# Causal masks added by VectorE in PSUM, and both 1024-row products in three parts from weights fetched in turn

## The chip, the cores and the metric

The kernel runs on one core of a Trainium2 chip. The metric is the device time of one execution in microseconds (us), from start to end, median of three runs.

## The reference

`x` is [64, 256, 256] and `ctx` is [64, 77, 256], all float32. For each of the 64 batches the reference computes two layers:

```
# layer 0: cross-attention over 77 keys, 16 heads of 64
n  = x * rsqrt(mean(x*x) + 1e-6) * norm_w
x  = x + softmax((n @ wq) (ctx @ wk)^T) (ctx @ wv) @ wo          # wo is [1024, 256]
# layer 1: causal attention, cross-attention, MLP; 16 heads of 16
x  = x + mha(ln1(x), ln1(x), causal=True) @ m_proj_w + m_proj_b
x  = x + mha(ln2(x), ctx,    causal=False) @ c_proj_w + c_proj_b
x  = x + relu(ln3(x) @ f_w1 + f_b1) @ f_w2 + f_b2                # f_w2 is [1024, 256]
```

In the causal attention a score whose key comes after its query is minus infinity before the softmax.

## The kernel before

A batch is cut into about a hundred **steps**, named as in the order table: `stat`, `norm`, `turn` (statistics, normalised rows, transposes), `q0 k0 v0` and `q1 k1 v1` (projections), `qs0` (layer 0 scores of one query tile and four heads, query rows down the partitions, for the softmax sums), `mt` (transposed shifts), `sk0` (the same scores with keys down the partitions, for the probabilities), `pv0` (probabilities times values), `wo` (output product, one of two row tiles); for the causal attention `qsA` and `qsB` (scores of query tile 0 and 1, for the sums), `skA` and `skB` (scores for the probabilities), `pv.1`, `proj.1`; for the third attention `qs2`, `sk2`, `pv.2`, `proj.2`; for the MLP `h.0` to `h.3` (256 hidden rows each) and `f2` (one of two row tiles). `ln.k` takes the logarithm of the sums of softmax k.

`LOOP_ORDER_TEXT` is one turn of the steady loop as a single row of steps. A turn works on three batches at once; the suffix `-` or `+` says that a step belongs to the older or to the younger of them. All engines walk this one row, each doing its own part of a step, so the row sets the order on TensorE (PE), ScalarE (ACT), VectorE (DVE) and GpSimd (POOL). 62 of the 64 batches' turns run in that loop; shorter rows fill and empty the pipeline.

The eight PSUM banks are dealt out in turn: a step takes the next one, two or four banks of the ring. `full[s]` counts what PE put into bank s and `free[s]` what was taken out; PE waits on `free` before it writes.

**Products.** float32 data goes through PE in one of two ways. `three` (lines 841 to 843) uses operands that were split into a high and a low float32r part and makes three matmuls. `plain_rows_product` (line 876) multiplies float32 as it is; the trace shows each such matmul as two. `wo` and `f2` use the plain way: eight k-slices of 128, each 128x128 by 128x256, for each of two row tiles. `wo0` and `wf2` lie in SBUF all the time; `coT` holds layer 0's attention output and, later in the turn, the hidden activations `hT`. ScalarE writes both: `pv0` by a copy from PSUM, `h` by a Relu with bias (line 575).

**Masks.** PE adds the causal mask to the scores by a bf16 matmul of an identity and a mask tile: line 958 after `qsA`/`qsB`, line 1009 ahead of `skA`/`skB`, one for each of the four banks of a step.

**Softmax sums.** DVE takes the maxima of a bank (line 701), ACT then exponentiates each head's piece with an accumulated sum (line 480, each followed by a read of the accumulator). The probabilities are plain exponentials of a whole bank (lines 549, 553, 557).

**Setup.** SP loads small tiles, `wk0`, `ck`, `wo0`, `f2`, and then the ten weights of `WEIGHTS` one after the other through two staging areas, where DVE splits them (lines 616 to 624). Nothing of the batches starts before DVE has given `consts_ready`.

## Time and profile before

| | |
|---|---|
| median of 3 runs | 5340.66 us (5338.04 to 5346.11) |
| the profiled execution | 5337.84 us, its span 5336.1 us |
| PE busy | 5106.7 us, 96% of the span |
| ACT busy | 4342.2 us, 81% |
| DVE busy | 2212.1 us, 41% |
| POOL busy | 536.4 us, 10% |
| granted TensorE clock | 0.993 of full speed |
| DMA | 67.10 MB, mean 13 GB/s |

Busy means that at least one instruction of the engine was under way. Matmuls are pipelined: a row in the trace lasts until its modelled end, while the next one starts earlier. What a kind of matmul costs PE is therefore read from the distance of the starts, and a duration is not added up.

### The profile page before, as it was taken

Reading aid. Unit: us, or ns where it says so; the run is one execution under the profiler, and the core shown is the slowest. Engines: PE = TensorE matmul, PEld = TensorE weight load, DVE = VectorE, ACT = ScalarE, POOL = GpSimd, SP = SyncE. Lnnn points to the kernel's source line nnn. Section 1 sums busy time; section 2 is a strip of 40 time slices with the busy share of each in tenths; the row PEclk is TensorE's granted clock in tenths of the full one; section 3 lists DMA queues with packets and bytes.
Section 4 is the critical chain, followed back from the end, with each engine's and each line's share of the span. In section 5 each row is a group of like instructions: output and inputs, shape, how many; then the busy total and the mean of one; then the engine's idle time right before and its main releaser. Section 6 shows DMA issues by size and latency. Waiting matters only on the chain.

```text
span 5336.1 us, 138120 instructions
## 1 busy us (share of the span) xinstructions
PE 5106.7 (96%) x48328; PEld 4133.6 (77%) x48328; DVE 2212.1 (41%) x5823; ACT 4342.2 (81%) x17665; POOL 536.4 (10%) x845
## 2 busy tenths in 40 slices
PE   6999999999999999999999999999999999999996
PEld 5777777787787777777777777877777777777775
DVE  3444444443444444444444444434444444444442
ACT  3888888888888888888888888888888888888884
POOL 0001011111111011010110111110110100101100
PEclk9999999999999999999999999999999999999998
DMA  2000000000000000000000000000000000000000
GB/s 76 12 8 14 13 8 13 13 8 13 12 9 13 10 11 13 8 13 13 8 14 13 8 14 13 8 13 10 11 13 8 13 13 8 14 13 7 14 8 5
DMA packets 64257, 67.10 MB, mean 13 GB/s; under 512 B 4593, under 2 KB 62769, under 8 KB 63921
## 3 DMA queue, kind: packets, MB, share of 16 engines
q1 hardware_dynamic: 63920, 64.19, 3.9%
q14 instruction: 318, 2.60, 0.2%
q8 instruction: 19, 0.31, 0.0%
HBM read 47.40 MB, written 16.78 MB: 12 GB/s over the span
## 4 chain that ended last, share of the span: by engine, by line
PE 62%; ACT 24%; DVE 6%; issue 6%; DMA 0%; DVEq 0%; POOL 0%; ACTq 0%; SPq 0%; PEldq 0%; PEld 0%; POOLq 0%
PE ps L876 17%; ACT ps L480 15%; PE ps L841 6%; PE ps L843 5%; PE ps L842 5%; PE ps L1048 5%; PE ps L1031 4%; ACT coT L575 3%; PE ps L1020 3%; PE ps L929 3%; PE ps L1009 2%; PE ps L997 2%; PE ps L939 2%; PE ps L1015 2%; ACT v L460 2%
## 5 line engine op out<-in xcount | busy, mean ns | idle before, releaser
L480 ACT ACTIVATE ps<-ps,negmax 128x77 f32<-128x77 f32 (+2 forms) x6144 | 2076.8, 397 | 197.0 <-DVE negmax L701 195.4
L480 ACT ACTIVATION_READ_ACCUMULATOR ps<-ps,negmax 128x1 f32 x6144 | 1617.6, 275 | 0.8
L701 DVE TENSOR_REDUCE negmax<-ps 128x4 f32<-128x308 f32 (+2 forms) x1792 | 923.5, 563 | 765.8 <-PE ps L939 381.3
L433 POOL TENSOR_TENSOR small<-small 128x1 f32<-128x1 f32 (+1 forms) x448 | 260.9, 582 | 4608.3 <-DVE small L675 2305.7
L696 DVE TENSOR_TENSOR zTl<-ps,zTh 128x256 fp32r<-128x256 f32 x512 | 199.3, 420 | 898.0 <-ACT zTh L460 898.0
L876 PE MATMUL ps<-wf,coT 128*128 128x256 f32 x2048 | 475.8, 386 | 46.4 <-ACT coT L575 46.4
L876 PEld LDWEIGHTS ps<-wf,coT 128*128 128x128 f32 x2048 | 379.8, 190 | 127.0 <-issue 80.2
L876 PE MATMUL ps<-wo,coT 128*128 128x256 f32 x2048 | 475.9, 385 | 0.0
L557 ACT ACTIVATE probs<-ps 128x512 f32<-128x512 f32 x768 | 394.9, 601 | 70.1 <-PE ps L1020 70.1
L876 PEld LDWEIGHTS ps<-wo,coT 128*128 128x128 f32 x2048 | 378.6, 190 | 66.7 <-issue 10.3
L549 ACT ACTIVATE probs<-ps 77x512 f32<-77x512 f32 x512 | 275.5, 588 | 182.2 <-PE ps L981 179.1
L929 PE MATMUL ps<-k0bd,q0T 128*128 128x154 f32 x2048 | 310.7, 299 | 0.0
L553 ACT ACTIVATE probs<-ps 77x512 f32<-77x512 f32 x512 | 254.6, 602 | 62.2 <-PE ps L997 62.2
L841 PE MATMUL ps<-xTh,hi_wq 128*128 128x256 f32 x1024 | 299.2, 292 | 1.5 <-DVE xTl L696 1.5
L841 PE MATMUL ps<-zTh,hi_f 128*128 128x256 f32 x1024 | 290.2, 283 | 1.0 <-issue 1.0
L843 PE MATMUL ps<-xTh,lo_wq 128*128 128x256 f32 x1024 | 287.4, 281 | 0.0
L842 PE MATMUL ps<-xTl,hi_wq 128*128 128x256 f32 x1024 | 286.8, 280 | 0.0
L843 PE MATMUL ps<-zTh,lo_f 128*128 128x256 f32 x1024 | 284.7, 278 | 0.0
L842 PE MATMUL ps<-zTl,hi_f 128*128 128x256 f32 x1024 | 284.7, 278 | 0.0
L929 PEld LDWEIGHTS ps<-k0bd,q0T 128*128 128x128 f32 x2048 | 277.2, 190 | 8.8
L981 PE MATMUL ps<-q0T,k0bd 64*77 64x256 f32 x2048 | 263.6, 376 | 0.0
L912 PEld LDWEIGHTS ps<-cT,wk 128*128 128x128 f32 x2048 | 243.4, 192 | 9.0
(181 smaller groups left out, 10798.5 us busy)
## 6 DMA issues: line engine op xcount, KB each, us to landing
xin<-x_dram SPq DMA_DIRECT2D x64, 256.0 KB, 2.7
x<-x_dram SPq DMA_DIRECT2D x64, 256.0 KB, 2.7
out<-xr SPq DMA_DIRECT2D x64, 256.0 KB, 2.3
cin<-ctx_dram SPq DMA_DIRECT2D x64, 77.0 KB
wk<-wk_dram SPq DMA_DIRECT2D x1, 1024.0 KB, 5.1
wo<-wo_dram SPq DMA_DIRECT2D x1, 1024.0 KB, 7.9
wf<-f_dram SPq DMA_DIRECT2D x1, 1024.0 KB, 10.3
probs<-wq_dram SPq DMA_DIRECT2D x1, 1024.0 KB, 9.6
```

Of the source, the lines that this page charges most:

```text
L433: nc.gpsimd.tensor_tensor(rstd[:, stage, ts], veps[:, stage, ts], minus_half[:, ts], ALU.pow).then_inc(rstd_ready[stage], 1)
L480: ins = nc.scalar.activation(scores, scores, ACT.Exp, bias=negmax[w][:, t, h:h + 1], accum_out=sums[w][:, t, h:h + 1])
L549: nc.scalar.activation(probs_slot(step, e)[0:S], bank(s)[0:S, :], ACT.Exp).then_inc(free[s], 1)
L557: nc.scalar.activation(probs_slot(step, r), bank(s), ACT.Exp).then_inc(free[s], 1)
L701: nc.vector.tensor_reduce(dst, bank(s)[:, 0:heads * width].rearrange("p (h k) -> p h k", h=heads), AX_X, ALU.max, negate=True).then_inc(ma ...
L841: pe.matmul(o, lh, rh, start=first, stop=False)
L842: pe.matmul(o, lh, rl, start=False, stop=False)
L843: return pe.matmul(o, ll, rh, start=False, stop=last)
L876: ins = pe.matmul(bank(s)[:, 0:C], src[:, k, t * P:(t + 1) * P], weight[:, k, :], start=(k == 0), stop=(k == kt - 1))
L929: ins = pe.matmul(bank(s)[:, j * 2 * S:(j + 1) * 2 * S], q0T[:, m, t * P:(t + 1) * P], k0bd[:, m, :, :], start=True, stop=True)
L981: ins = pe.matmul(bank(s)[0:S, j * T:(j + 1) * T], k0bd[es, m, e, :], q0T[es, m, :], start=False, stop=(j == 1), skip_group_check=True)
L1048: ins = pe.matmul(bank(s)[rows, 0:T], lhs, p, start=(e == 0), stop=(k == 2 and e == 1), skip_group_check=True)
```

## The change

1. **Masks.** The mask matmuls go. DVE adds the mask tile to the scores in PSUM, in place, bank by bank (`mask`): before the maxima in `qsA` and `qsB` (semaphore `chain`), before ACT's exponential in `skA` and `skB` (semaphore `masked`).
2. **Both 1024-row products in three parts.** `wo` and `f2` become `tail_product`, which uses `three`. Their left operands are split: `coTh` and `coTl`. For `pv0`, ACT writes the high part and DVE the low one; for `h`, DVE makes both parts and ACT has no share any more. The two weights, split, no longer fit side by side: one pair of tiles `tail_h`, `tail_l` holds one of them at a time. Setup splits both and stores the parts in DRAM (`parted`); in every turn POOL fetches 2 MB of `f2` parts after `wo.1`, and 2 MB of `wo` parts after `f2.1`. The Relu is max(y, -bias) with the bias moved into the row that `f2` adds.
3. **Orders.** A new order of steps; ACT and DVE get orders of their own, in which the parts of a step (a bank, a mask `m0` to `m3`, a half of `h`) are placed singly.
4. **Banks.** Each step names its banks in the table (`:4156`), in place of the ring.
5. Layer 0's probabilities get four slots in place of eight. SP's loads follow the order of steps. One turn of the loop is written out, so the loop runs 61 times.

```diff
-    mt.0- rms+ pv.1.1 sk0.3- proj.1.1 proj.1.0 sk0.1- sk0.2- sk0.0- stat.2.0 stat.2.1 norm.0+ norm.2.0
...
+mt.0-:7 pv.1.1:1 sk0.1-:23 proj.1.1:6 proj.1.0:1 stat.2.0 sk0.0-:75 stat.2.1 norm.2.0 norm.2.1 rms+ pv0.1-:2
...
+def signals(order):
...
-        wo0 = sb("wo0", [P, M0, C])
-        wf2 = sb("wf2", [P, MF, C])
+        tail_h, tail_l = sb("tail_h", [P, M0, C], F32R), sb("tail_l", [P, M0, C], F32R)
...
+            def store_parts(n, value):
+                i = [m for m, _, _ in WEIGHTS].index(n)
+                sp.wait_ge(w_free[i % 2], i // 2 + 1)
+                sp.dma_start(parted[n][0], tail_h[:].bitcast(F32)).then_inc(parts_out, 16)
+                sp.dma_start(parted[n][1], tail_l[:].bitcast(F32)).then_inc(parts_out, 16)
+                sp.wait_ge(parts_out, value)
...
+            def load_parts(kind):
+                n = "wo0" if kind == "wo" else "f2"
+                nc.gpsimd.dma_start(tail_h[:], parted[n][0]).then_inc(tail_in[kind], 16)
+                nc.gpsimd.dma_start(tail_l[:], parted[n][1]).then_inc(tail_in[kind], 16)
...
+                    if n in ("wo", "f2") and (n, 1 - step[1]) in c.seen:
+                        done = {s: v for st in order if st[0] == n for s, v, _ in c.of[st]["bank"]}
+                        for s, v in done.items():
+                            pool.wait_ge(full[s], v)
...
+                        nc.gpsimd.tensor_tensor(passed[:], minus_half[:], minus_half[:], ALU.mult)
+                        if later:
+                            load_parts(later[0])
...
+            def mask(u, r, heads, tile, at, added):
+
+                s, v, _ = u["bank"][r]
+                dve.wait_ge(full[s], v)
+                scores = bank(s).rearrange("p (h k) -> p h k", h=heads)[:, :, at:at + P]
+                nc.vector.tensor_tensor(scores, scores, tile[:].unsqueeze(1).to_broadcast([P, heads, P]),
+                                        ALU.add).then_inc(added, 1)
...
+                            ins = nc.vector.tensor_scalar(hTh[:, k, :], bank(s)[:, m * T:(m + 1) * T],
+                                                          minus_bias[:, k:k + 1], None, ALU.max)
...
+                            ins = nc.vector.scalar_tensor_tensor(out=hTl[:, k, :], in0=bank(s)[:, m * T:(m + 1) * T],
+                                                                 scalar=minus_bias[:, k:k + 1],
+                                                                 in1=hTh[:, k, :].bitcast(F32), op0=ALU.max,
+                                                                 op1=ALU.subtract)
...
-            def plain_rows_product(u, weight, src, kt, t):
+            def tail_product(u, th, tl, t):
                 s = take_bank(u)
-                for k in range(kt):
-                    ins = pe.matmul(bank(s)[:, 0:C], src[:, k, t * P:(t + 1) * P],
-                                    weight[:, k, :], start=(k == 0), stop=(k == kt - 1))
+                ts = slice(t * P, (t + 1) * P)
+                for k in range(M0):
+                    ins = three(bank(s)[:, 0:C], th[:, k, ts], tl[:, k, ts], tail_h[:, k, :], tail_l[:, k, :],
+                                k == 0, k == M0 - 1)
                 ins.then_inc(full[s], 1)
...
-                        for s, _, _ in u["bank"]:
-                            heads = 4 if n == "qsA" else 2
-                            diagonal = bank(s).rearrange("p (h k) -> p h k", h=heads)[:, :, 512 // heads - P:]
-                            pe.matmul(diagonal, identb[:], causal[:].unsqueeze(1).to_broadcast([P, heads, P]),
-                                      start=False, stop=True, skip_group_check=True).then_inc(full[s], 1)
```

**Three places in the loop.** On DVE, behind the statistics of the layer norm ahead of the MLP (`stat.3`). Before, the rows there are:

```order
L665 BN_STATS stats<-xs 128x6 [waits free0]
L660 REGISTER_ALU
L669 BN_AGGR mv<-stats 128x2 [waits chain]
L660 REGISTER_ALU
L678 TENSOR_SCALAR small<-mv 128x1 [waits chain]
L682 REGISTER_ALU
L687 TENSOR_SCALAR z<-xs,mv,small 128x256 [waits rstd_ready1]
L682 REGISTER_ALU
L687 TENSOR_SCALAR z<-xs,mv,small 128x256 [waits rstd_ready1]
L694 REGISTER_ALU
L696 TENSOR_TENSOR zTl<-ps,zTh 128x2x128 [waits hi_done]
L694 REGISTER_ALU
```

They are the statistics, the two normalised tiles (`z`) and the low parts of their transposes. Now there stand:

```order
L760 BN_STATS stats<-xs 128x6 [waits free2]
L755 REGISTER_ALU
L764 BN_AGGR mv<-stats 128x2 [waits chain]
L755 REGISTER_ALU
L773 TENSOR_SCALAR small<-mv 128x1 [waits chain]
L805 REGISTER_ALU
L806 TENSOR_REDUCE negmax0<-ps 128x4 [waits full1]
L804 REGISTER_ALU
L806 TENSOR_REDUCE negmax1<-ps 128x2 [waits full4,chain]
L777 REGISTER_ALU
L782 TENSOR_SCALAR z<-xs,mv,small 128x256 [waits rstd_ready1]
L796 REGISTER_ALU
```

Between the second statistics and its normalised tile there are now a `qs0` maximum and a `qsB` one, and masks follow.

On PE, around the first tile of `f2` (`L929` and `L1061` are `qs0` scores). Before:

```order
L929 MATMUL ps<-k0bd,q0T 128x154 [waits free4,free1]
L929 MATMUL ps<-k0bd,q0T 128x154
L876 MATMUL ps<-wf2,coT 128x256 [waits free4,free2,free3,free1]
L876 MATMUL ps<-wf2,coT 128x256 x7
L837 REGISTER_ALU
L1009 MATMUL ps<-identb,causal 128x2x128 [waits free3,free7]
L1009 MATMUL ps<-identb,causal 128x2x128 [waits free4]
L1009 MATMUL ps<-identb,causal 128x2x128 [waits free5]
L1009 MATMUL ps<-identb,causal 128x2x128 [waits free6]
L1015 MATMUL ps<-maxT1,head_of32 128x256 x8
```

Now:

```order
L1061 MATMUL ps<-k0bd,q0T 128x154 [waits free0,free2]
L1061 MATMUL ps<-k0bd,q0T 128x154
L225 REGISTER_ALU
L1061 MATMUL ps<-k0bd,q0T 128x154 [waits free0,free3,free7]
L1061 MATMUL ps<-k0bd,q0T 128x154
L1206 ISA [waits free5,free3]
L972 MATMUL ps<-tail_h,coTh 128x256 [waits free6,f2_in]
L973 MATMUL ps<-tail_l,coTh 128x256
L974 MATMUL ps<-tail_h,coTl 128x256
L972 MATMUL ps<-tail_h,coTh 128x256
```

The plain matmuls and the mask matmuls of `skA` behind them are gone; `f2` waits for the fetched weights (`f2_in`) and for the banks that DVE frees.

On POOL, where `wo.1` ends. Before:

```order
L433 TENSOR_TENSOR small<-small 128x1 [waits stat_ready2]
L452 TENSOR_TENSOR x1<-x1,row 128x256 [waits norm_ready2]
L432 REGISTER_ALU
L433 TENSOR_TENSOR small<-small 128x1 [waits stat_ready2]
L452 TENSOR_TENSOR x1<-x1,row 128x256 [waits norm_ready2]
L432 REGISTER_ALU
```

Now:

```order
L517 TENSOR_TENSOR small<-small 128x1 [waits stat_ready2]
L548 ISA
L548 ISA [waits full1]
L553 TENSOR_TENSOR passed<-small 128x2 [waits full0]
L522 DMA tail_h<-parted_f2 128x2048
L523 DMA tail_l<-parted_f2 128x2048
L544 TENSOR_TENSOR x1<-x1,row 128x256 [waits norm_ready2]
```

Ahead of the row additions POOL now waits until both `wo` tiles are in their banks and issues two DMAs.

## Rows read from the trace of the kernel before

**Rows 1.** Page, part 1: busy us (share of span) xinstructions.

```profile
span 5336.1 us, 138120 instructions
...
PE 5106.7 (96%) x48328; PEld 4133.6 (77%) x48328; DVE 2212.1 (41%) x5823; ACT 4342.2 (81%) x17665; POOL 536.4 (10%) x845
```

**Rows 2.** Busy us by engine in a turn, from `qsA` to `skB`, and behind `qs2.1`.

```profile
core 0: us, PE busy (x) PEld busy (x) DVE busy (x) ACT busy (x) POOL busy (x), PEclk, DMA share, GB/s
2674.24:2755.36 81.12, 79.07 (x758) 64.04 (x754) 34.12 (x90) 67.73 (x276) 8.33 (x13) 1.00 0.03 11
2713.09:2745.26 32.17, 30.98 (x280) 25.11 (x278) 14.96 (x34) 28.65 (x125) 2.50 (x4) 1.00 0.01 3
2690.53:2702.68 12.15, 12.15 (x88) 10.88 (x85) 6.91 (x21) 11.10 (x67) 1.84 (x3) 1.00 0.00 1
```

**Rows 3.** Timeline, SP: start us, us, engine line op; one turn apart.

```profile
2674.24 0.40 SPq L400 DMA_DIRECT2D out<-xr  x1
...
2755.36 0.40 SPq L400 DMA_DIRECT2D out<-xr  x1
```

**Rows 4.** Timeline, PE: start, us, operation xcount [idle before <-releaser].

```profile
2715.40 0.28 PE L841 MATMUL ps<-hi_cp,zTh 128*128 128x256 f32 x1
...
2716.46 0.28 PE L841 MATMUL ps<-hi_mv,z1Th 128*128 128x256 f32 x1
...
2727.58 0.61 PE L958 MATMUL ps<-causal,identb 128*128 128x256 bf16 x4
2727.94 0.37 PE L841 MATMUL ps<-zTh,hi_f 128*128 128x256 f32 x1
...
2737.40 3.69 PE L876 MATMUL ps<-wf,coT 128*128 128x256 f32 x16 [0.73 <-ACT coT L575]
2740.93 0.60 PE L1009 MATMUL ps<-identb,causal 128*128 128x256 bf16 x4
2741.45 0.51 PE L1015 MATMUL ps<-maxT,head_of 32*128 32x256 f32 x8
...
2742.76 1.04 PE L1009 MATMUL ps<-identb,causal 128*128 128x512 bf16 x4
2743.72 0.67 PE L1015 MATMUL ps<-maxT,head_of 32*128 32x128 f32 x16
...
2745.26 2.37 PE L929 MATMUL ps<-k0bd,q0T 128*128 128x154 f32 x16
```

**Rows 5.** Timeline, all engines, softmax sums behind `qs2.1`, up to its `mt.2`.

```profile
2691.13 0.30 ACT L480 ACTIVATE ps<-ps,negmax 128x77 f32<-128x77 f32 x1 [0.65 <-DVE negmax L701]
...
2701.41 0.23 ACT L542 ACTIVATE logs<-sums 128x32 f32<-128x32 f32 x1 [0.37 <-ACT ps L480]
...
2702.16 0.29 DVE L755 TENSOR_TENSOR mparts<-negmax,mparts 128x128 fp32r<-128x128 f32 x1
...
2702.68 0.38 PE L965 MATMUL ps<-ident,mparts 128*128 128x128 f32 x2
```

**Rows 6.** Groups by line and form: xcount | busy us, mean ns | idle before.

```profile
L696 DVE TENSOR_TENSOR zTl<-ps,zTh 128x256 fp32r<-128x256 f32 x512 | 199.3, 420 | 898.0 <-ACT zTh L460 898.0
...
L696 DVE TENSOR_TENSOR xTl<-ps,xTh 128x512 fp32r<-128x512 f32 x64 | 44.2, 691 | 51.6 <-ACT xTh L460 51.6
...
L557 ACT ACTIVATE probs<-ps 128x512 f32<-128x512 f32 x768 | 394.9, 601 | 70.1 <-PE ps L1020 70.1
...
L575 ACT ACTIVATE coT<-ps,bias_h 128x256 f32<-128x256 f32 x512 | 192.8, 485 | 6.3 <-PE ps L843 6.3
```

**Rows 7.** DMA issues: KB each, us to landing.

```profile
wo<-wo_dram SPq DMA_DIRECT2D x1, 1024.0 KB, 7.9
wf<-f_dram SPq DMA_DIRECT2D x1, 1024.0 KB, 10.3
```

**Rows 8.** Timeline, setup: last weight split, ACT's table load behind `consts_ready`.

```profile
49.48 0.76 DVE L624 SCALAR_TENSOR_TENSOR lo_cp<-probs,hi_cp 128x256 fp32r<-128x256 f32 x2
...
53.44 1.28 ACT L586 ACT_TABLE_LOAD   x1 [53.44 <-DVEq L654]
```

More of the change, by code:

```diff
@@ L17 @@
 MASKED = -1e30
-RINGS = {"bank": 8, "split": 1, "chain": 1, "max": 1}
+RINGS = {"bank": 8, "split": 1, "chain": 1, "max": 1, "masked": 1}
 FIRST = 24
@@ new lines @@
+skA.0/1 skA.0/2 skA.0/0 skA.0/3 skB/3 skB/0 skB/1 skB/2 qs0.1.1 qs0.1.0 ln.0 pv.1.0 skA.1/3 skA.1/2 skA.1/1
+skA.1/0
+"""
+DVE_ORDER_TEXT = """
+pv.1.1 proj.1.1 proj.1.0 stat.2.0 stat.2.1 norm.2.0 pv0.1 norm.2.1 rms turn.2.1 pv0.0 turn.2.0 norm.0 pv0.3
+pv0.2 qs2.1/3 qs2.1/1 qs2.1/2 turn.0 qs2.1/0 wo.0 stat.1.0 qs2.0/2 qs2.0/3 qs2.0/0 qs2.0/1 wo.1 norm.1.0
+stat.1.1 ln.2 norm.1.1 turn.1.0 turn.1.1 pv.2.0 pv.2.1 ctx qsA/m0 qsA/0 qsA/m3 qsA/m1 qsA/3 qsA/1 qsA/m2
+proj.2.0 stat.3.0 qsA/2 qsB.0/m3 qsB.0/m2 qsB.0/m0 qsB.0/3 qsB.0/2 qsB.0/m1 qsB.0/0 norm.3.0 proj.2.1
@@ L52, in steps, with step_of @@
+stat.3.1 qs0.1.2 qsB.0/1 norm.3.1 qsB.1/m1 qsB.1/1 qsB.1/m3 qsB.1/3 turn.3.1 turn.3.0 qsB.1/m0 qsB.1/m2
+qs0.0.2 qs0.0.0 qsB.1/0 qsB.1/2 h.2/0 h.2/1 h.0/0 qs0.0.1 ln.1 qs0.1.3 h.0/1 h.1/0 qs0.0.3 h.1/1 skA.0/m1
+skA.0/m2 skA.0/m0 skA.0/m3 h.3/0 h.3/1 skB/m3 skB/m0 skB/m1 skB/m2 qs0.1.1 qs0.1.0 f2.0 ln.0 pv.1.0 skA.1/m3
+skA.1/m2 skA.1/m1 skA.1/m0 f2.1
+"""
+def step_of(word):
+    name, *numbers = word.split(".")
+    return (name, *map(int, numbers))
 def steps(text):
-    order, stages = [], {}
+    order, stages, banks = [], {}, {}
@@ L54, in steps, with parts_of @@
     for word in text.split():
-        name, *numbers = word.rstrip("+-").split(".")
-        step = (name, *map(int, numbers))
+        word, _, taken = word.partition(":")
+        step = step_of(word.rstrip("+-"))
         order.append(step)
         stages[step] = {"+": 2, "-": 0}.get(word[-1], 1)
-    return order, stages
-LOOP_ORDER, STAGES = steps(LOOP_ORDER_TEXT)
+        banks[step] = [int(c) for c in taken]
+    return order, stages, banks
+def parts_of(text):
+    items = []
+    for word in text.split():
+        word, _, part = word.partition("/")
+        items.append((step_of(word), int(part) if part.isdigit() else part))
+    return items
@@ L113 @@
 CARRIED = [(p, step) for step in LOOP_ORDER for p in sources(step) if (STAGES[p] + 1) % 3 < (STAGES[step] + 1) % 3]
-def slot_uses(order):
-    total = {r: sum(USES[step[0]].get(r, 0) for step in order) for r in RINGS}
-    return {r: [(total[r] - s + n - 1) // n for s in range(n)] for r, n in RINGS.items()}
+def signals(order):
+    inside = set(order)
+    given = {r: [] for r in RINGS}
+    for step in order:
+        assert len(BANKS[step]) == USES[step[0]].get("bank", 0)
+        given["bank"] += [(step, j, s) for j, s in enumerate(BANKS[step])]
+    for step, _ in ACT_ORDER:
+        if step in inside and "split" in USES[step[0]]:
+            given["split"].append((step, 0, 0))
+    for step, part in DVE_ORDER:
+        uses = USES[step[0]]
+        if step not in inside:
+            continue
+        if "masked" in uses:
+            given["masked"].append((step, int(part[1:]), 0))
+        elif str(part).startswith("m"):
+            given["chain"].append((step, int(part[1:]), 0))
+        elif "max" in uses:
+            given["max"].append((step, part or 0, 0))
+        elif "chain" in uses and part != 1:
+            given["chain"] += [(step, j, 0) for j in range(uses["chain"])]
+    return given
@@ L151, in all @@
-    def all(self, order):
-        for step in order:
-            self.next(step)
-        return self
+        self.after = after
+        self.of = {step: {"place": k, **{r: [None] * n for r, n in USES[step[0]].items()}} for k, step in enumerate(order)}
+        self.seen = set()
+        for ring, given in signals(order).items():
+            at = [0] * RINGS[ring]
+            for step, j, s in given:
+                at[s] += 1
+                value, total = before[ring][s] + at[s], sum(before[ring]) + sum(at)
+                if per_turn is not None:
+                    value = turn * per_turn[ring][s] + value
+                    total = turn * sum(per_turn[ring]) + total
+                self.of[step][ring][j] = (s, value, total)
```

285 lines of the change are left out of this document (156 added, 129 removed).

## Prediction

> **What bounds the kernel now.** I read the page's busy shares first: PE is busy for 96% of the span, ACT for 81%, DVE for 41% [rows 1]. The span is 5336.1 us. Next comes the period of the steady loop. The store of a finished batch is issued once a turn, and two of these issues stand 81.12 us apart [rows 3], so 62 turns make 5029 of the 5336 us. The window of such a turn says how full it is: PE 79.07 us, ACT 67.73, DVE 34.12, at full clock [rows 2]. PE lacks work for 2.05 us of a turn. That is a PE bound, with ACT 13 us behind it. Busy shares over a turn hide where ACT is as good as full, though, so I looked at two stretches. From `qsA` to `skB` (32.17 us) PE is busy for 30.98 and ACT for 28.65; 1.19 of PE's 2.05 us of waiting lie here, 0.73 of them ahead of `f2.0`, which waits for ACT's Relu [rows 2, 4]. Behind `qs2.1` (12.15 us up to `mt.2`) PE is never idle, but the chain it would wait for next ends just in time: the last `mparts` is written at 2702.45, `mt.2` starts at 2702.68 [rows 2, 5].
>
> **The change part by part.** All terms are per turn, against 81.12 us.
>
> *Tail products.* One tile of `f2` costs PE 3.53 us (2737.40 to 2740.93) [rows 4]; four tiles make 14.1. In three parts, a k-slice is three matmuls; such slices start 0.353 us apart (2715.40 to 2716.46 is three of them, with data as the stationary operand as here) [rows 4]. 4 tiles x 8 slices x 0.353 = 11.3. PE saves 2.8 us.
>
> *Mask matmuls.* A group of four 512 wide takes PE 0.96 us (2742.76 to 2743.72), one 256 wide between 0.36 (2727.58 to 2727.94) and 0.52 (2740.93 to 2741.45) [rows 4]. Two of the first and four of the second kind at 0.44: 3.7 us saved.
>
> PE's own work falls from 79.07 to 72.6 us. With the waits of today the turn would be 74.6 us.
>
> *ACT* loses `h`: 192.8 us over 64 batches, 3.0 a turn [rows 6]. The copy of `pv0` becomes a rounding copy of the same size. ACT's work becomes 64.7 us.
>
> *DVE* gains masks (8 of 512 columns at 0.69 us, 16 of 256), the two parts of `h` (16 of 256), and `pv0`'s low parts (4 of 512). 256 columns are 0.42 us singly and 0.38 in a row (two in 0.76) [rows 6, 8]. 12 x 0.69 + 32 x 0.38 = 20.4; DVE reaches 54.5 us. Its in-place adds in PSUM are in no row of before; I price them by the subtractions that read PSUM and write SBUF, and bound them by 0.34 (half) and 1.0 us for 512 columns.
>
> So over a whole turn PE stays the fullest. The two stretches decide.
>
> *The stretch from `qsA` to `skB`.* The new order has the same steps here except that `f2.0` comes behind it, and four more `qs0` and one `q0` come into it. PE: 30.98 - 3.53 - masks 3.2 (two 512, three 256) + 2.4 for four `qs0` [rows 4] + 1.4 for a `q0` (twelve matmuls of 0.118) = 28.1 us. ACT: 28.65 - 3.0 + 16 exponentials of 77 columns + 0.6 for `q0`'s copy + 2.1 for `skB`'s four. The 77-wide ones run at 0.31 us (32 of them from 2691.13 to 2701.04, which is 0.37 before the logarithm) [rows 5], so 5.0; `skB`'s are 394.9/768 = 0.51 each [rows 6]. Sum 33.3. DVE: 14.96 + masks 8 x 0.69 + 12 x 0.38 + `h` 16 x 0.38 + four maxima at about 0.4 = 32.7. Both are longer than PE. `f2.0` needs `h.3`'s low part, which DVE makes after all of this except `skB`'s masks (2.8): not before 29.9, plus about 1 us before DVE has its first bank of `qsA`. So PE waits 1.8 us at least and some 2.9 with that lag, most of it at the new order's `turn.3` (DVE's normalised tile stands behind two maxima), `mt.1` and `f2.0`. Within DVE's 32.7 us no further gap is allowed for; with `chain` waits between a mask and its maximum I get up to 4.0. I take 2.7, nearer to the bare sum, since steps can slip past each other, where 1.19 stood.
>
> *Behind `qs2.1`.* PE's 12.15 us become 12.15 - 1.4 (two `wo` tiles) + about 0.2 (`turn.1.0`) = 10.9. The chain (maxima, 32 exponentials, logarithm, `mparts`) is untouched and took 2690.53 to 2702.45, 11.9 us [rows 5]. PE now waits 1.1 us where it waited 0. Bounds: 0 if ACT finds its scores earlier, 1.5.
>
> *Elsewhere* the waits stay: 2.05 - 1.19 = 0.86.
>
> Period: 72.6 + 2.7 + 1.1 + 0.86 = 77.2 us, 3.9 less. 62 turns: -242 us. The two batches' worth of work outside the steady turns save PE's 6.5 each: -13.
>
> *Weight fetch.* The store of a batch is issued at 2674.24, and `wo.0` starts at 2690.53 [rows 2, 3], 16.3 us later; `f2.1` ended some 0.8 us ahead of the store (DVE's add of 0.42 and two hand-overs), so there are 17.1 us for a fetch in the place of before, and 15.7 after, since one `q0` is moved out. The second of two 1 MB loads landed 7.9 us after its issue, the third 10.3 [rows 7]. Two loads by POOL then need about 8 to 10 us plus POOL's own work of 1 to 3. I cost it at nothing, under cover of those 15.7 us; each us beyond them costs 62. The `f2` fetch has over 35 us. POOL's row additions behind `wo.1` come later by its issue time, ahead of work that PE needs several us later: nothing. The loads are issued by POOL and change dtype to float32r. The Trainium skill, "DMA: Bandwidth & Descriptors", section "SWDGE vs HWDGE vs iDMA", has it that GpSimd writes the descriptors into SBUF rings and can be locked out of them by VectorE's two-port mode, which would speak against a fetch by POOL beside a busier VectorE; the same page ("Anatomy of one DMA") gives 2.0 us plus bytes over 436 GB/s, an estimate of 6.8 us for both MB, by which the fetch would be early. No row of before shows a DMA of POOL's, so neither can be weighed here, and the sum would be the same by the second.
>
> *Setup.* Splitting two more weights: 2 x 8 slices x 2 parts at 0.38 = 12 us at most [rows 8]; storing one's parts before the other may be split: 8 (two 1 MB, as the 7.9 row); bias rows and the wait for a load: 4; two 1 MB loads fewer ahead of the first weight: -5. Sum +19, between 8 and 30. All of it lies ahead of the first batch.
>
> Span: 5336.1 - 242 - 13 + 19 = 5100. The median of before is 4.6 above the profiled span, so I predict **5105 us**.
>
> **The rivals.**
>
> *The waits don't grow.* If the new orders and the fixed banks let ACT and DVE run ahead, PE waits for 2 us as before and the turn is 74.6: 5336 - 404 - 13 + 19 + 5 = 4943. For it: ACT and DVE are full in one stretch only. Against it: `f2.0` can't start before DVE's 29.9 us are done. Chance 13%.
>
> *DVE becomes the bound.* Mask, maximum and `h` stand in one row on DVE; if an in-place add costs 1.0 us in place of 0.69, eight of 512 and twelve of 256 columns add about 4 us to the stretch, nearly all onto PE: 62 x 4 = 248, 5353 at the worst and 5200 to 5330 for half or more of it. Chance 13%.
>
> *The fetch comes late (slower).* `wo.0` waits for `wo_in`. The gain of a turn is 3.9 us, and the cover is 15.7, so a fetch of about 19.5 us, or 2 MB at some 0.12 MB/us behind 3 us of issue, eats it all (setup's 19 us included). At 24 us the run takes 5105 + 62 x 8.3 = 5620; at 21 us, 5434. For it: a converting DMA by POOL is in no row, and a batch's store and the next loads of `x` run beside it. Against: 1 MB more lands 2.4 us later in the rows [rows 7], over twice as fast. Chance 7%. That is also the point of the page's lock-out rule above: it would end here.
>
> *The change doesn't do what it says*, for instance a three-part slice slower here than in `proj` because its four operands differ: each 0.05 us on 32 slices is 1.6 us a turn, 100 us in all. It is part of the upper range.
>
> **How the numbers follow.** Forecast (5000 to 5200): 64%. No growth of waits (4900 to 5000): 13%. DVE as the bound, or the fetch late by 2 to 4 us (5200 to 5345): 13 and 2%, the last 2 of them within 0.2% of before. Slower: 7%, and 1% below 4900. The range leaves a tenth on either side: 4960 to 5230. A measurement of this kernel can tell 0.2%, 11 us. Faster 0.91, same 0.02, slower 0.07.
>
> **What would show it.** The period between stores: 77.2 us. PE busy 72 to 73 us of it. Tail slices 0.35 us apart. PE waiting for `z` or `mparts` 1 to 2 us, and ahead of `f2.0` and `mt.2` about 1 us. No wait of PE on the fetched tiles; the fetch landing 9 to 13 us after `f2.1`. `consts_ready` near 72 us in place of 53. The prediction is wrong if PE's waits in a turn are below 3 or above 6.5 us, or if PE waits for `tail_h` or `tail_l` at all.

## The result and the profile after

| | before | changed |
|---|---|---|
| median, us | 5340.3 (5338.0 to 5346.1) | 5423.0 (5414.8 to 5432.7) |
| profiled execution, span | 5336.1 | 5412.8 |
| period between two stores | 81.12 | 81.2 to 83.0, once 86.95; mean of 56 turns 82.00 |

The changed kernel takes 1.0154 times the time of before, 95% interval 1.0135 to 1.0173: it is slower by 1.5%, where 4.4% faster was forecast, and outside the range.

The page of the changed kernel, its first part; it answers to [rows 1]:

```profile
span 5412.8 us, 150595 instructions
## 1 busy us (share of the span) xinstructions
PE 4987.1 (92%) x48856; PEld 4045.3 (75%) x48856; DVE 3385.0 (63%) x8681; ACT 4158.5 (77%) x17153; POOL 695.8 (13%) x1230
```

Two turns that follow each other, each from one issue of a store to the next. The columns are the window and its length, then busy us (and instructions) of each engine, TensorE's granted clock, DMA share and GB/s; they answer to [rows 2]:

```profile
core 0: us, PE busy (x) PEld busy (x) DVE busy (x) ACT busy (x) POOL busy (x), PEclk, DMA share, GB/s
2638.47:2719.65 81.18, 76.44 (x767) 62.30 (x763) 52.25 (x134) 64.81 (x268) 10.80 (x20) 1.00 0.18 63
2719.65:2802.46 82.81, 77.91 (x767) 62.96 (x763) 52.24 (x134) 65.02 (x268) 10.81 (x20) 0.98 0.17 62
```

Three things stand in these rows. PE's own work is 76.4 us at full clock where the sum had 72.6. PE waits for 4.7 us of the first turn (81.18 - 76.44), as the sum had it (4.66). And the second turn is 1.6 us longer, nearly all of it PE's work at a lower clock; every second or third turn is of that kind.

What PE waited for, over the whole run (total us, times, longest), is not what had been forecast:

```profile
PE ps L980 <- DVE z L782: 115.7, 65, 4.6
PE ps L1085 <- ACT ps L583: 50.6, 65, 3.8
PE ps L1093 <- DVE mparts L867: 46.9, 66, 7.2
```

The first of them, the transposes of `turn.2.1`, wait for `z`: 1.7 to 1.9 us a turn. In the kernel before, the transposes waited 23.0 us for `z` in the whole run:

```profile
PE ps L849 <- DVE z L687: 23.0, 69, 3.2
```

The cause of this wait is found by going back from engine to engine. GpSimd's timeline from `f2.1`'s end on:

```profile
start us, us, engine line op out<-in xcount [idle before <-releaser]
2719.24 0.59 POOL L522 DMA_DIRECT2D tail_h<-parted_wo  x1
2719.83 0.54 POOL L523 DMA_DIRECT2D tail_l<-parted_wo  x1
2725.55 0.56 POOL L517 TENSOR_TENSOR small<-small 128x1 f32<-128x1 f32 x1 [5.18 <-DVE small L773]
2728.44 0.72 POOL L540 TENSOR_TENSOR xr<-xs,row 128x256 f32<-128x256 f32 x1 [2.33 <-DMA out<-xr]
2729.12 0.54 POOL L517 TENSOR_TENSOR small<-small 128x1 f32<-128x1 f32 x1
```

SyncE's, VectorE's and TensorE's in the same stretch:

```profile
2719.65 0.40 SPq L482 DMA_DIRECT2D out<-xr  x1
...
2729.70 0.81 DVE L782 TENSOR_SCALAR z<-xs,mv,small 128x256 f32<-128x256 f32 x1 [2.30 <-POOL small L517]
...
2730.56 0.69 PE L980 MATMUL ps<-ident,z 128*128 128x128 f32 x2 [1.89 <-DVE z L782]
2731.18 0.71 PE L1103 MATMUL ps<-maxT,head_of 64*77 64x256 f32 x4
2731.69 1.91 PE L1109 MATMUL ps<-q0T,k0bd 64*77 64x256 f32 x8
```

The batch's store is issued 0.41 us after GpSimd's first load, beside 2 MB. It lands 8.6 us after its issue. The output tile `y` is the tile `xr`, so GpSimd may not write the next batch's `xr` until the store is done (2728.44), and the inverse root for the second row tile stands behind that on GpSimd's queue (2729.12). VectorE's `z` waits for the root, PE for `z`. The page's DMA issues (KB, median us from issue to landing), answering to [rows 7], and below them the store's line in the page of before:

```profile
tail_h<-parted_wo POOLq DMA_DIRECT2D x64, 1024.0 KB, 5.7
tail_l<-parted_wo POOLq DMA_DIRECT2D x64, 1024.0 KB, 8.3
out<-xr SPq DMA_DIRECT2D x64, 256.0 KB, 8.6
```

```profile
out<-xr SPq DMA_DIRECT2D x64, 256.0 KB, 2.3
```

Behind that gap the clock falls. Windows of the same turn, same columns:

```profile
2719.65:2729.60 9.95, 8.88 (x94) 5.50 (x86) 3.77 (x11) 5.28 (x11) 2.44 (x5) 1.00 0.74 264
2729.60:2731.60 2.00, 1.04 (x6) 0.71 (x8) 1.72 (x6) 0.31 (x1) 0.76 (x2) 0.74 0.00 0
2731.60:2733.20 1.60, 1.60 (x12) 0.84 (x8) 1.56 (x6) 0.06 (x1) 0.71 (x1) 0.50 0.00 0
```

A granted clock of 0.50 is 1.2 GHz, the lower of the two levels; the eight matmuls at 2731.69 last 1.91 us, where 1.02 is usual.

### The profile page after: what moved, and what is told of

Read it like the earlier page. It is cut to its first block and busy times, and to the rows that moved or that the text cites. A ratio compares the mean times of both kernels' runs of the same rounds, so it can differ in the third digit from the quotient of the medians.

```text
span 5412.8 us, 150595 instructions
## 1 busy us (share of the span) xinstructions
PE 4987.1 (92%) x48856; PEld 4045.3 (75%) x48856; DVE 3385.0 (63%) x8681; ACT 4158.5 (77%) x17153; POOL 695.8 (13%) x1230
## 5 line engine op out<-in xcount | busy, mean ns | idle before, releaser
L972 PE MATMUL ps<-tail_h,coTh 128*128 128x256 f32 x2048 | 601.7, 294 | 20.9 <-DVE coTl L791 16.3
L973 PE MATMUL ps<-tail_l,coTh 128*128 128x256 f32 x2048 | 575.6, 281 | 0.0
L974 PE MATMUL ps<-tail_h,coTl 128*128 128x256 f32 x2048 | 574.9, 281 | 0.0
L972 PEld LDWEIGHTS ps<-tail_h,coTh 128*128 128x128 f32 x2048 | 385.4, 188 | 66.8 <-issue 66.8
L798 DVE TENSOR_TENSOR ps<-ps,causal 128x256 f32<-128x256 f32 (+1 forms) x768 | 370.5, 513 | 81.2 <-PE ps L1085 81.0
L1061 PE MATMUL ps<-k0bd,q0T 128*128 128x154 f32 x2048 | 363.9, 305 | 25.7 <-DVE zTl L791 16.3
L974 PEld LDWEIGHTS ps<-tail_h,coTl 128*128 128x128 f32 x2048 | 386.4, 189 | 0.0
L973 PEld LDWEIGHTS ps<-tail_l,coTh 128*128 128x128 f32 x2048 | 385.9, 188 | 0.0
L1061 PEld LDWEIGHTS ps<-k0bd,q0T 128*128 128x128 f32 x2048 | 286.7, 190 | 78.7 <-DVE zTl L791 30.7
L798 DVE TENSOR_TENSOR ps<-ps,causalT 128x256 f32<-128x256 f32 (+1 forms) x768 | 339.7, 509 | 4.8 <-PE ps L1143 4.8
L563 ACT CAST zTh<-ps 128x256 fp32r<-128x256 f32 x512 | 194.9, 401 | 137.6 <-PE ps L980 124.6
L791 DVE TENSOR_TENSOR coTl<-ps,coTh 128x512 fp32r<-128x512 f32 x256 | 176.3, 689 | 196.0 <-ACT coTh L563 194.1
```

What stands on the lines that cost most here:

```text
L791: nc.vector.tensor_tensor(lo, src, hi, ALU.subtract).then_inc(free[s], 1)
L798: nc.vector.tensor_tensor(scores, scores, tile[:].unsqueeze(1).to_broadcast([P, heads, P]), ALU.add).then_inc(added, 1)
L972: pe.matmul(o, lh, rh, start=first, stop=False)
L973: pe.matmul(o, lh, rl, start=False, stop=False)
L974: return pe.matmul(o, ll, rh, start=False, stop=last)
L1061: ins = pe.matmul(bank(s)[:, j * 2 * S:(j + 1) * 2 * S], q0T[:, m, t * P:(t + 1) * P], k0bd[:, m, :, :], start=True, stop=True)
```

## The experiments

The words "theory A" in the expectations mean this chain: fetch, late store, late root, gap, lower clock.

### Store ahead of the fetch, and no fetch at all

The first adds one wait to GpSimd's queue:

```
                         for s, v in done.items():
                             pool.wait_ge(full[s], v)
+                        if n == "f2" and later:
+                            pool.wait_ge(y_stored, b * 16 + 32)
```

> The changed kernel with one wait more: after f2.1, GpSimd issues the fetch of wo0's parts only when the store of that batch has landed. Theory A (the fetch delays the store, the store delays GpSimd's xr add, that delays z, the gap lets TensorE's clock fall): the store lands in 2 to 3 us as before and not 8.6, GpSimd's wait for it (133.0 us in the run of the changed kernel) goes below 20 us, TensorE's wait for z (115.7 us) below 50, and the turns of 82.6 to 82.9 us come down to the 81.2 to 81.6 of their neighbours: 0.7 to 1.5 us a turn, 5330 to 5380 us. Rival B (the loss is in TensorE's own instructions, 76.4 us of them a turn where 72.6 were forecast; z is late for other reasons): the store is quick and the time stays within 10 us of 5423.

The second fetches once; both products then use the parts of `wo`, and `f2`'s are left out:

```
-                        if later:
-                            load_parts(later[0])
...
-                        pe.wait_ge(tail_in["f2"], b * 32 + 32)
+                        pe.wait_ge(tail_in["wo"], 32)
```

> The changed kernel with the parts fetched once, before the first batch; both products use wo0's parts, so f2's product has the wrong weights (that work is the same in size). All that the fetches do to the time is gone. Theory A: as with the store ahead, 5330 to 5380 us, not below it by more than 10 us, since no TensorE wait was for a fetched tile. Rival C (4 MB a turn on the DMA engines and in SBUF slow the matmuls themselves): TensorE's own time falls below 75.5 us a turn and the whole to 5250 to 5320. Rival B: within 10 us of 5423.

Measured: 5244.6 us with the store ahead, 0.9822 of the kernel before (0.9806 to 0.9839), and 5242.6 us without fetches (0.9803 to 0.9835). The two are the same. The expectations had the mechanism and too small a gain: it is 178 us, where 5330 to 5380 us had been expected, a gain of 43 to 93. A turn of the first:

```profile
2719.40:2798.84 79.44, 76.18 (x767) 62.31 (x763) 52.30 (x134) 64.65 (x268) 10.84 (x19) 1.00 0.18 64
```

GpSimd's timeline, where the loads now start 2.5 us after the store's issue and the `xr` addition stands between the roots without a wait:

```profile
2721.92 0.59 POOL L522 DMA_DIRECT2D tail_h<-parted_wo  x1
2725.61 0.56 POOL L517 TENSOR_TENSOR small<-small 128x1 f32<-128x1 f32 x1 [2.56 <-DVE small L775]
2726.15 0.72 POOL L540 TENSOR_TENSOR xr<-xs,row 128x256 f32<-128x256 f32 x1
2726.84 0.59 POOL L517 TENSOR_TENSOR small<-small 128x1 f32<-128x1 f32 x1
```

The store in its page's DMA issues, and PE's wait for `z` in its list of waits:

```profile
out<-xr SPq DMA_DIRECT2D x64, 256.0 KB, 2.4
```

```profile
PE ps L982 <- DVE z L784: 9.4, 4, 4.6
```

The wait for `z` gave 106 us, PE's busy time 56 (4987.1 to 4931.5), most of the rest small waits. So the fetch, placed beside the store, cost the changed kernel 178 us, and none of it through the tiles that it loads. Over 56 turns the mean period falls from 82.00 to 79.23 us: 1.8 us less of waits, 0.9 less of PE's busy time. Without the fetches altogether nothing more is gained, so the traffic by itself doesn't slow this kernel.

### Register instructions

Each bank of PSUM has a semaphore whose wait value grows by the bank's uses in a turn. In the kernel before five banks have 13 uses and three have 12, and banks share the registers that hold these values. With banks set by step the uses run from 10 to 15. PE runs 88 register instructions a turn where it had 37. The edit makes the last use of a bank count for more, so that all banks advance alike:

```
+    if len(order) == len(LOOP_ORDER):
+        uses["bank"] = [max(uses["bank"])] * len(uses["bank"])
...
-                ins.then_inc(free[s], 1)
+                ins.then_inc(free[s], ADDED[s])   # 1, at a bank's last use 1 + what is missing
```

> The changed kernel; the last use of each bank in a turn of the loop adds as much to the bank's semaphores as brings all banks to the same count a turn, so that the wait values of the banks share registers again. Register instructions in the loop: TensorE 35 instead of 88, VectorE 78 instead of 98, ScalarE 59 instead of 93; nothing else differs. Rival B (TensorE's own time grew by 3.8 us a turn partly through 51 more register instructions in its stream): TensorE's own time falls by 1 to 1.5 us a turn, the whole to 5330 to 5360 us. Theory A alone: register instructions are hidden in TensorE's queue, and the time stays within 10 us of 5423.

The other way round, in the kernel before:

```
+    uses["bank"] = [a + s for s, a in enumerate(uses["bank"])]
```

> The kernel before; the last use of bank s in a turn adds s to its semaphores on top, so that no two banks share wait values. Register instructions in the loop: TensorE 97 instead of 37, VectorE 67 instead of 53, ScalarE 101 instead of 52. The counterpart of the run with even counts. Rival B: 1 to 1.7 us a turn more, 5400 to 5450 us. Theory A alone: within 10 us of 5340.

And even counts with the store ahead:

> The store ahead of the fetch and even counts together (register instructions of TensorE 35 a turn instead of 88). If the register instructions cost what they gave back in the run with even counts (16 us) and took in the kernel before (25 us), whatever else goes on: 5220 to 5230 us, with TensorE's own time 0.25 to 0.4 us a turn below the 76.2 us it has with the store ahead. Rival: those 16 us came out of the clock's fall and not out of TensorE's stream, then 5240 to 5248.

Measured: 5407.1 us for the first (1.0131, 1.0114 to 1.0148), 16 less than the changed kernel; 5363.0 for the second (1.0048, 1.0031 to 1.0065), 25 more than before; 5207.8 for the third (0.9755, 0.9738 to 0.9771), 37 less than with the store ahead alone. None of the three lies where either theory had it. Register instructions in PE's stream are not free here: 53 to 60 of them a turn go with 0.4 to 0.6 us. The edits change the number for ScalarE and VectorE too, but the time is in PE's own work: in the kernel before it rises from 79.1 to 79.7 us a turn, and PE's waits fall from 2.0 to 1.8. The 16 us of the first run are fewer, and the likely reason is that there nearly every turn has the lower clock behind the gap (81.8 to 82.2 us from the eleventh turn to the fifty-second), where with uneven counts some escape it. A turn of the third run:

```profile
2621.34:2699.97 78.63, 75.59 (x770) 61.28 (x766) 52.17 (x134) 64.83 (x268) 10.86 (x19) 1.00 0.19 65
```

PE's own work is 75.6 us, 0.6 less than in the row of the store ahead; the waits stay at 3.1 (means of 56 turns: 3.05 and 3.07). **This version, 5207.8 us, is the fastest that was found and beats both kernels.**

### What the two edits are worth

Masks undone, on top of the store ahead (VectorE's mask parts are dropped from its order, and the lines of before come back):

```
-                            nc.vector.tensor_tensor(scores, scores, tile..., ALU.add)
+                            pe.matmul(diagonal, identb[:], causal..., start=False, stop=True)
```

> With the store ahead, and TensorE adding the causal mask again by 24 matmuls a turn, VectorE none; orders and banks as in the changed kernel. If the masks' term of the prediction stands (3.7 us of TensorE a turn, of it some 1 us given back as waits): 2.7 to 3.7 us a turn more, 5410 to 5475 us, TensorE's own time near 79.9 a turn. Rival: TensorE gains less than 3 us, because the first matmul of a step pays for its start in any case: below 5410.

Measured: 5323.9 us (0.9976, 0.9966 to 0.9987), 79 us or 1.3 a turn above the run with the store ahead. The rival was right. The turn:

```profile
2756.69:2837.24 80.55, 78.67 (x794) 63.86 (x790) 42.42 (x110) 64.58 (x268) 10.85 (x19) 1.00 0.18 63
```

PE's own work is 2.5 us more than without mask matmuls (78.67 against 76.18), not 3.7, and PE waits for 1.9 us and not 3.1. So VectorE's masks save 2.5 and give 1.2 back as waits.

Tails undone, first with fetches (on the store ahead), then without:

```
-                    ins = three(bank(s)[:, 0:C], th[:, k, ts], tl[:, k, ts], tail_h[:, k, :], tail_l[:, k, :], ...)
+                    ins = pe.matmul(bank(s)[:, 0:C], th[:, k, ts].bitcast(F32), tail_h[:, k, :].bitcast(F32), ...)
```

> With the store ahead, and both 1024-row products in one float32 matmul a slice of the high parts (the fetches stay; no low parts are made or used, so the two products are those of the rounded values, which leaves out VectorE's 8 subtractions a turn). If the tails' term stands (2.8 us a turn): 5400 to 5420 us. If it is the 2.35 us read from the trace of the changed kernel: 5385 to 5395. Rival: the three-part product brings nothing once VectorE's low parts and the longer way to f2 are counted: within 15 us of 5244.

> The run without fetches (5242.6 us), with both 1024-row products in one float32 matmul a slice of the high parts (left out: the fetches, f2's own weights, and VectorE's 8 low parts a turn). The run that undid the tails with the fetches in place took 5612.0 us, with 2.15 us stalls of TensorE for no releaser at the head of the turn, beside the fetch. Theory: those stalls belong to the fetch landing beside them, and the tails alone are worth 2.2 to 2.8 us a turn: 5380 to 5420 us. Rival: the plain product itself costs that much (fewer matmuls before the loop's end, so TensorE comes to the next turn's instructions sooner): 5550 us or more here too.

Measured: 5612.0 (1.0516, 1.0498 to 1.0533) and 5614.1 us (1.0507, 1.0489 to 1.0524), some 370 us above their bases, 6 a turn. Both theories missed; the rival of the second run had the time, and its reason, the next turn's instructions, fits what follows. With no fetch on the chip the stall is the same, so it isn't the fetch. PE's timeline without fetches, in its first step after `mt.0`, and the row of its waits; behind it the clock is at 0.66 and 0.50 for two windows of 2 us:

```profile
2738.92 0.38 PE L1164 MATMUL ps<-probs,v 128*32 128x256 f32 x1 [0.23 <-issue]
2741.45 1.50 PE L1164 MATMUL ps<-probs,v 128*32 128x256 f32 x12 [2.15 <-issue]
...
PE ps L1164 <- issue: 139.2, 120, 2.4
```

In the tile sums of the timelines the product itself costs what was expected: 3.65, 3.37, 3.54 and 3.72 us for four tiles in plain form, against 3.03, 2.94, 3.02 and 2.95 in three parts, 2.3 us a turn. The other 3.7 us are the stall and the clock behind it.

The profile names no releaser for the stall, but the pages show what goes with it. One of the queues that bring instructions carries 565 packets (9.26 MB) in both runs, where it has 26 in the changed kernel and in both bases. The page of the run without fetches, then that of its base:

```profile
q8 instruction: 565, 9.26, 0.7%
```

```profile
q8 instruction: 26, 0.43, 0.0%
```

The 539 packets more are nine for each of 60 turns. One other version has this, the masks on VectorE in the old order below: 358 packets, 25 in its base. There the stall comes in 37 of 62 turns, and each of these 37 has nine packets beside it; the turns without the stall have none, but for the last two at the loop's end (6 and 5). So the stall is most likely the loading of PE's own instructions at the head of the loop. No run tested this by itself, and why these three versions, which have the fewest matmuls of all (46808), load them again and again isn't shown.

### The orders

ScalarE and VectorE through the steps in PE's order, on store ahead and even counts; the two order texts are made from `LOOP_ORDER_TEXT`, a step's parts together:

```
-DVE_ORDER_TEXT = """ ... ctx qsA/m0 qsA/0 qsA/m3 qsA/m1 qsA/3 qsA/1 qsA/m2 proj.2.0 stat.3.0 qsA/2 ...
+DVE_ORDER_TEXT = """ ... ctx qsA/m0 qsA/m1 qsA/m2 qsA/m3 qsA/0 qsA/1 qsA/2 qsA/3 ...
```

> Store ahead and even counts (5207.8 us), but ScalarE and VectorE work through the steps in TensorE's order, all parts of a step together, a step's four masks ahead of its four maxima. The run in the old order took 6394.8 us, and it had both the old order and one order for all engines. Theory: it is the one order for all engines that costs there, since VectorE now stands between TensorE and ScalarE at the masks: 5600 us or more. Rival: the old order of TensorE was at fault: below 5350.

Measured: 6699.5 us (1.2537, 1.2516 to 1.2558), 1492 us more, at a granted clock of 0.885 over the run, as the theory had it (5600 or more). The new order of PE is of use only with the separate orders of ScalarE and VectorE.

The rest was done in PE's order of before (with `sk0` and `pv0` interleaved, since `probs0` has half the slots), one order for all engines, banks in turn, store ahead:

```
-    norm.2.1 turn.0+ turn.2.0 turn.2.1 pv0.2- pv0.1- pv0.0- pv0.3- q1.2 ...
+    norm.2.1 turn.0+ pv0.3- sk0.1- turn.2.0 turn.2.1 pv0.2- sk0.0- pv0.1- pv0.0- q1.2 ...
```

> With the store ahead, all arithmetic of the changed kernel, but TensorE's order that of the kernel before (only sk0 and pv0 interleaved, since probs0 has half the slots), banks taken in turn, and ScalarE and VectorE in TensorE's order. Theory: the new order breaks up runs of like steps and makes TensorE's own 76.2 us a turn out of the 72.6 that the prediction's edits give; in the old order it is 73 to 74. Its waits are then longer than the 3.0 us of the new order, as ScalarE and VectorE aren't arranged for it: 5 to 8 us. Together 5180 to 5330 us. Rival: TensorE's own time is as high in this order (75.5 or more), so that its growth has another cause, and the time is 5300 to 5450.

> The old order for all engines (that of the run of 6394.8 us) with both edits undone: masks by TensorE, both 1024-row products in one float32 matmul a slice of the high parts (left out: their low parts and VectorE's 8 low parts a turn; the fetches stay). It is the kernel before but for sk0 and pv0 interleaved, relu on VectorE and the fetches. If these three are small: 5330 to 5450 us. If the interleaved sk0 and pv0 are themselves what makes TensorE wait for coT: 5700 or more. It is the base for the next two.

> The same old order with the masks on VectorE alone added. Prediction's term: 3.7 us a turn off TensorE and 1.5 more of waits, so 100 to 150 us below the run with neither. Theory now: on the way from qsA to the maxima a bank's mask (0.69 us) stands ahead of its maximum (0.69), ScalarE starts later, and in an order made without this TensorE's waits grow by more than the mask matmuls took, and the clock falls in them: 300 us or more above the run with neither.

> The same old order with the three-part products (and VectorE's low parts) alone added, masks by TensorE. Prediction's term: 2.8 us a turn off TensorE, 150 us below the run with neither. Theory now: TensorE's own time falls by 2.2 us a turn, but pv0 and h now pass through ScalarE and VectorE one after the other before wo and f2, in front of which TensorE has nothing else in this order: the time is within 60 us of the run with neither, or above it.

| in the old order | us | ratio to before (interval) |
|---|---|---|
| neither edit | 5677.6 | 1.0634 (1.0616 to 1.0652) |
| masks on VectorE | 6185.7 | 1.1556 (1.1484 to 1.1628) |
| three-part tails | 5952.2 | 1.1154 (1.1136 to 1.1173) |
| both | 6394.8 | 1.1981 (1.1961 to 1.2001) |

The run with both missed its expectation by over 1000 us, and the one with neither fell between its two. Each edit alone makes that order slower, by 508 and 275 us, as the last two theories had it. Of the 508, some 120 go with the stall beside instruction packets: the 37 turns that have it take 95.7 us (median), the others 92.3. In the new orders, with the store ahead, each edit makes the kernel faster, by 79 and 367 us, and of the 367 only some 145 (2.3 a turn) are the product; the rest is the stall of the version that undoes it. So what an edit is worth depends on the order in which it stands. Even the small move of `sk0` and `pv0`, with relu on VectorE and the fetches, costs 340 us: PE then waits for VectorE's relu ahead of `f2` (115.7 us in the profiled run) and the clock is 0.977 to 0.983 over the runs.

Like steps in a row, in the kernel before:

```
-    norm.2.1 turn.0+ turn.2.0 turn.2.1 pv0.2- pv0.1- pv0.0- pv0.3- q1.2 ...
+    norm.2.1 pv0.2- turn.0+ pv0.1- turn.2.0 pv0.0- turn.2.1 pv0.3- q1.2 ...
-    ... ln.1- h.0 h.3 h.1 h.2 qs0.0.3+ qs0.1.3+ mt.1- qs0.0.0+ qs0.1.0+ f2.0 ...
+    ... ln.1- h.0 qs0.0.3+ h.3 qs0.1.3+ h.1 qs0.0.0+ h.2 mt.1- qs0.1.0+ f2.0 ...
```

> The kernel before, with its four pv0 steps and its four h steps no longer in a row: other steps that stand beside them (turn.0, turn.2.0, turn.2.1, and qs0.0.3, qs0.1.3, qs0.0.0) are put between them; no work is added. Theory (a change from one kind of step to another costs TensorE about 0.1 us, which is where 2 to 3 us a turn of the new order's own time come from): 9 more changes of kind, 0.6 to 1.2 us a turn, 5375 to 5415 us. Rival (like steps in a row are no cheaper): within 10 us of 5338.

Measured: 5814.8 us (1.0879, 1.0861 to 1.0898), 471 more; both expectations missed. The time didn't go where the test looked. PE's timeline at `f2.0`, which has lost the steps that covered ScalarE's Relu, and then the row of its waits:

```profile
2797.58 0.69 PE L929 MATMUL ps<-k0bd,q0T 128*128 128x154 f32 x4
2803.69 0.77 PE L876 MATMUL ps<-wf,coT 128*128 128x256 f32 x1 [5.42 <-ACT coT L575]
```

```profile
PE ps L876 <- ACT coT L575: 338.9, 64, 5.4
```

Behind those 5.42 us the clock stays at 0.50 for 6 us. The longer wait (5.42 where [rows 4] have 0.73), the clock and the starts read off below make up the 7.6 us a turn. The disturbed run still answers its question in its undisturbed stretch. Before, four `pv0` in a row, and `cq` behind them:

```profile
2683.21 3.67 PE L1031 MATMUL ps<-probs,v 77*64 77x256 f32 x32
2686.82 0.39 PE L841 MATMUL ps<-zTh,hi_cq 128*128 128x256 f32 x1
```

Split, all at full clock:

```profile
2745.06 1.08 PE L1031 MATMUL ps<-probs,v 77*64 77x256 f32 x8
2746.08 0.44 PE L849 MATMUL ps<-ident,z 128*128 128x128 f32 x2
2746.45 1.08 PE L1031 MATMUL ps<-probs,v 77*64 77x256 f32 x8
2747.46 0.44 PE L849 MATMUL ps<-ident,z 128*128 128x128 f32 x2
2747.83 1.08 PE L1031 MATMUL ps<-probs,v 77*64 77x256 f32 x8
2748.95 0.38 PE L841 MATMUL ps<-zTh,hi_cq 128*128 128x256 f32 x1
```

In a row the four take 3.61 us from start to start; alone they take 1.02, 1.02, 1.01 and 1.12, 4.17 in all (the first isn't shown). The four `h` go from 5.55 to 5.95. So a step that stands alone costs PE 0.1 to 0.2 us more than one behind its like, which is the size that the theory had.

### Two tries at the longest wait left

PE's largest wait with even counts is for bank 6 at `qsB.0` (54.6 us, 0.80 a turn). First its four parts were renamed so that this bank is asked for last (for ScalarE and VectorE part 3 is now 0, 2 is 1, 0 is 2 and 1 is 3):

```
...
-qsB.0-:6437
+qsB.0-:7346
...
```

> Store ahead and even counts, with qsB.0's four parts renamed so that the bank that qsA's second part frees last (bank 6) is asked for last and not first; ScalarE and VectorE keep their orders in time. TensorE waits 0.80 us a turn for that bank (54.6 us of the run). If that wait shrinks to the one matmul that needs it: 0.3 to 0.6 us a turn less, 5170 to 5190 us. Rival: the four parts end when bank 6 is free in any case and the next wait grows by as much: 5200 to 5210.

Then ScalarE was given that part sooner:

```
...
-ctx qsA/0 k0.1 qsA/3 qsA/1 k0.0
+ctx qsA/0 qsA/3 k0.1 qsA/1 k0.0
...
```

> Store ahead and even counts (5207.8 us), with ScalarE taking qsA's fourth part before k0.1 and not after: bank 6, for which TensorE waits 0.80 us a turn at qsB.0, is then free some 0.5 us sooner, if VectorE's maximum is there. Theory: the wait shrinks by 0.3 to 0.5 us a turn, 5175 to 5195 us. Rival (as with the renamed parts, which made 210 us of loss out of a wait moved to qsB.1): a later wait grows past 1 us, the clock falls to its half behind it, 5300 or more.

Measured: 5417.8 us (1.0139, 1.0122 to 1.0156), 210 more, and 5229.3 us (0.9798, 0.9781 to 0.9814), 22 more; all four expectations missed. In the second the wait shrank to 19.7 us, as meant, and another for a bank grew from 15.9 to 38.6. The sum of PE's waits fell by 0.3 us a turn and its busy time rose by 0.6, which no row here explains.

In the first the wait for bank 6 is gone from `qsB.0`'s rows, but not from the time. The eight matmuls of `qsB.0` take 1.84 us to the next step's start, where they took 1.07 behind a wait of 0.80: PE now waits inside the step, and the profile counts that as busy.

```profile
2770.77 1.90 PE L1102 MATMUL ps<-k1bd,q1T 32*128 32x512 f32 x8
2772.61 0.39 PE L989 MATMUL ps<-hi_cp,zTh 128*128 128x256 f32 x1
```

And a long wait now stands at `qsB.1`, 6 us behind one of 0.36:

```profile
2775.38 0.43 PE L989 MATMUL ps<-hi_wv,cTh 128*77 128x512 f32 x1 [0.36 <-ACT ps L600]
...
2781.57 1.12 PE L1102 MATMUL ps<-k1bd,q1T 32*128 32x512 f32 x2 [1.39 <-ACT ps L600]
```

```profile
2775.00:2783.00 8.00, 6.09 (x28) 3.18 (x28) 4.96 (x13) 6.52 (x29) 1.25 (x2) 1.00 0.00 0
2783.00:2787.00 4.00, 4.00 (x22) 4.00 (x21) 2.41 (x7) 3.13 (x12) 0.00 (x0) 0.57 0.00 0
```

PE is busy for 6.09 of the 8 us ahead of the fall, and then runs 4 us at a granted 0.57. The turn is 3.3 us longer. The clock's share is about 1.7 us (4 us at 0.57, or 0.980 over a turn of 81.9 us), and the other half is the new wait of 1.39 us and small ones.

## Why the prediction was wrong

The forecast had 77.2 us a turn, the changed kernel takes 82.0: 4.8 more. The run with the store ahead (79.2) splits this: 2.8 us by the fetch, 3.6 of PE's own work (76.2 where 72.6 were forecast), and 1.6 less of waits than had been forecast (3.1 and not 4.66).

**The fetch costed at nothing: the step that failed.** The prediction took 15.7 us of cover for the tile's reader, and that was right: both parts land 5.7 and 8.3 us after their issue, and PE waits at no time for `tail_h` or `tail_l`. What I left out is who else is on the way at that moment. I had written that a batch's store runs beside the fetch, and used it only to ask whether the fetch would be late. The store is late, 8.6 us where it took 2.3, and `y` being `xr` hands that on. Price: 1.8 us of waits a turn, nearly all the gap ahead of `turn.2.1`, and 0.9 of PE's busy time, most of it the clock: 2.8 of the 4.8, and the whole sign. Without it the change gives 5244.6 us, 1.8% faster than before. That is still 140 us above the forecast and outside the range, and the rest is the step that follows. Neither of the two signs that were to show the prediction wrong (PE's waits outside 3 to 6.5 us in a turn, a wait for the fetched tiles) came: they watched the reader of the tiles, and not the store.

The estimate of 6.8 us for both MB, made from the Trainium skill, "DMA: Bandwidth & Descriptors", section "Anatomy of one DMA", is short of what the traces show: the second part lands 8.9 us after the first's issue, and 7.9 with the store ahead. That section says nothing of a store beside the loads.

**PE's own work, 72.6 forecast, 76.2 measured with the store ahead.** This is the second step that failed; the prediction had only its first two terms. Of these 3.6 us:

- *Masks*, 3.7 forecast, 2.5 measured (experiment): 1.2. I had added up the distances of the mask matmuls. Without them the steps' own matmuls start dearer: `skA.0`'s take 1.48 us in the run with the store ahead, and 1.30 behind their masks in the run that undid them.
- *Tails*, 2.8 forecast, 2.2 measured: 0.6. A tile of 24 matmuls takes 2.94 to 3.03 us, so slices are 0.355 apart as forecast, plus the step's start; the four tiles make 11.9 us, and I had 11.3.
- *Register instructions*, no term: 0.6 (experiment). The notion that banks set by step change only waits was wrong.
- *Broken rows*, no term: 0.55 for `pv0` (3.61 to 4.16) and 0.6 for `h` (5.55 to 6.12), by the timelines of before and of the run with the store ahead. That splitting alone costs about so much is shown for `pv0`, less fully for `h`: its slices start 0.36 us apart in the new kernels, with even counts too, and 0.34 in the kernel before, but 0.35 there with uneven counts. So a part of this may be the register term counted twice; no run tells.

They make 3.5 of the 3.6. The terms were measured in different versions, so that they add up this closely is in part luck. I treated the diff's new order as a matter of waits only.

**PE's waits, 4.66 forecast, 4.7 in the turn at full clock and 4.9 on average.** The sum agrees, and by luck: 1.8 of it is the gap that wasn't foreseen. The rest is 3.1, so the three terms that I had (2.7, 1.1 and 0.86) were 1.6 too high together. PE never waits ahead of `f2.0`. From `qsA` to `skB` it waits for 1.3 us (0.29, 0.72 and 0.26 in the run with the store ahead), and not 2.7.

**DVE and ACT.** 54.5 and 64.7 forecast, 52.3 and 64.8 measured. DVE was no bound. A mask of 512 columns in place takes 0.69 us, as priced.

**Setup.** 19 us forecast; `consts_ready` comes at 68.9 us where it came at 53.4, 15.5 more.

**The rivals.** The late fetch had 7%. It said "slower", and for another reason than the one that came: it asked whether `wo.0` would wait. The gain that would have to be eaten was 3.9 us a turn; in truth the change had 1.9 in hand (81.12 to 79.23), and 2.8 came.

## What to carry to other kernels

When a transfer is added under cover, list what else is issued in the same microseconds, who waits for each of those, and which tiles alias; a large load belongs behind a small store that gates the next batch, and one semaphore wait may settle it. When steps are put into a new order, count PE's cost of starts and the registers that the wait values need, not the waits alone. And on a kernel whose PE is 96% busy price a wait by what the clock does behind it: here 1.4 us in one place took 1.7 us more by the clock, and 0.8 in another took nothing, so an edit is worth trying only with the order that is made for it. Where PE stops and the profile names no releaser, look at the packets of the instruction queues.
